# Turned probabilities through one PSUM bank, row sums by a column of ones, values in two banks

## The chip, the cores and the metric

The kernel runs on one core of one Trainium2 chip. The core has a matrix engine (PE, with its weight loads, PEld), a vector engine (DVE), a scalar engine (ACT), a general engine (Pool) and a DMA-issuing engine (SP); each takes its own instructions in order, and they wait for one another by semaphores. The metric is the time of one execution in microseconds; lower is better.

## The reference, cut to what matters

Two layers of gated cross attention, each with a mixture of experts behind it, on `x` (16 batches of 112 tokens, 256 wide) and a context of 375 keys per batch. The change lies in the first layer alone:

```
x = x + tanh(g_xattn[0]) * L0_xattn(layernorm(x), ctx, mask, ...)   # 16 heads of 16
    q = query @ Wq.T + bq ; k = key @ Wk.T + bk ; v = key @ Wv.T + bv
    scores = q * scale @ k.T + (1 - mask) * -10000
    probs  = softmax(scores)                 # over 375 keys
    ctx    = probs @ v                       # [112, 16] per head
x = x + tanh(g_ffn[0]) * L0_ffn(layernorm(x), ...)   # top 2 of 8 experts
```

The second layer (16 heads of 64 over 487 keys) and the last experts follow and are not touched.

## The kernel before, in words

The program has three stages, one after the other: small heads (with the first experts), large heads, and the experts of the second layer. The first, `phase_attention_small_heads`, runs over 16 batches, and each batch over 16 heads. One head is one slot `s` of the loop in `body`, which every engine has for itself. In slot `s` of batch `b`:

- PE: `scores(s)` into one of two banks `ps_s` (L593); `transposes(s-2)`, three fp32 transposes of 125 keys each of the probabilities into one of two banks `ps_t` (L602); `values(s-4)`, six products of turned probabilities and v, each split into a high and a low half in fp16, into the one bank `ps_o` (L616); then the slot's work items: projections of batch b+1 (`PSLOT`: keys in slots 0 and 1, turned tokens in 2, queries in 4, values in 5 to 7; L509, L531) and expert products of batch b-1 (`DSLOT`: slots 7 to 14, the four pairs of experts in 9, 10, 12 and 13; L509, L562, L569, L576).
- DVE: `maxima(s)` adds the mask, scales and takes the row maximum (L837); copies for the items; `plo(s-2)` writes the low half of the turned probabilities out of `ps_t` (L842).
- ACT: items; `exps(s-1)` (L701), with the row sum by the accumulator of the instruction; `phi(s-2)` writes the high half out of `ps_t` (L708).
- Pool: normalisation, splits of queries and context into halves, the residual, sums of experts, in one list per batch. SP: loads, the rearranging copies `stack_keys` and `mask_queries`, stores, in one list per batch.

Heads lag by slots, so in slot `s` a negative `s - lag` means a head of the batch before. `transposes(h)` wait for `exps(h)` and, for their bank, for `plo(h-2)`. `values(b, 0)` would fall in slot 4, but `ps_o` still holds batch b-1 until `read_out(b-1)` in slot 4; PE defers it to slot 5, which does two heads. `read_out` divides later by the sums that the accumulator gave. Batch 0 has no expert items; batches 14 and 15 have a copy of the next stage's weights (`next_high`) on ACT in half of their slots. After the last batch a short drain does the transposes and values that are left. The order of work is written out by hand.

Of the kernel before, what the change touches and what calls it, by code (L numbers as in the profile page):

```python
# [16 lines left out]
ALU = mybir.AluOpType  # L17
# [8 lines left out]
B = 16  # L26
T = 112
# [12 lines left out]
KB0, NB0 = 125, 3  # L40
SCALE0 = D0 ** -0.5
# [71 lines left out]
def phase_attention_small_heads(nc, x, ctxT, mask, g_xattn, g_ffn, wq, wk, wv, bq, bk, bv, wg, we, be, consts,  # L113
# [3 lines left out]
    with ExitStack() as ctx:  # L117
# [47 lines left out]
        v_s = [sb(f"v_s{i}", [128, NB0, H, 2, D0], F16) for i in range(2)]  # L165
# [3 lines left out]
        prob = sb("prob", [T, RING, C], F32)  # L169
        top = sb("top", [T, RING], F32)  # L170
        sums = [sb(f"sums{i}", [T, H], F32) for i in range(2)]
        pT = sb("pT", [128, RING, 2, NB0, 128], F16)
# [38 lines left out]
        s_blank = sem("blank")  # L211
# [80 lines left out]

        def heads(s, lag, b, par):

            h = s - lag
            return (b, par, h) if h >= 0 else (b - 1, 1 - par, h + H)


# [6 lines left out]
        def _(sp):  # L305
# [60 lines left out]
            def body(b, par):  # L366
                if ahead(b, 1):
                    load_mask(b + 1, 1 - par)
                if not first(b):
                    load_residual(b - 1)  # L370
                if ahead(b, 2):
                    load_tokens(b + 2)
                if ahead(b, 1):
                    stack_keys(b + 1, 1 - par)
                    mask_queries(b + 1, 1 - par)
                clear_rows(b)
                if not ahead(b, 1):
                    load_residual(b)
                if not first(b):
                    store(b - 1)  # L380
# [5 lines left out]
            sp.wait_ge(s_blank, 1)  # L386
            run_batches(sp, body)
            store(B - 1)
# [5 lines left out]
        def _(pool):  # L394
            pool.memset(be_f[:, :], 0.0).then_inc(s_zero, 1)
            pool.memset(blank[:, :], 0.0).then_inc(s_blank, 1)
# [4 lines left out]
            settled = (s_zero, 4)  # L401

            def split_context(c):

                need_all(pool, settled, (s_cload, 16, c, 16), (s_item, PI, c, 0))
                pool.tensor_copy(ctx_s[:, HI, :, :], ctx_f[:, :, :]).then_inc(s_csplit, 1)
                need(pool, s_csplit, 2, c, 1)
                pool.tensor_tensor(ctx_s[:, LO, :, :], ctx_f[:, :, :], ctx_s[:, HI, :, :], ALU.subtract).then_inc(s_csplit, 1)
# [26 lines left out]
            def residual(c):  # L435

                need(pool, s_rload, 16, c, 16)
                pool.tensor_tensor(x_b[:, :], x_res[:, :], bv_t[:, :], ALU.add).then_inc(s_xb, 1)
                need(pool, s_rsumt, 1, c, 1)
                need(pool, s_oread, 1, c, 1)  # L440
# [16 lines left out]
            def sum_experts(c, alone=True):  # L457

                for j in range(E // 2):
                    if not alone:  # L460
                        for n in range(2):
                            next_low((c - (B - 3)) * 8 + 2 * j + n)
                    need(pool, s_scaled, E // 2, c, j + 1)
                    need(pool, s_odd if j else s_x2, E // 2 if j else 1, c, j)
                    pool.tensor_tensor(acc_odd[:, :], scaled[j % 2][:, :], (acc_odd if j else x1)[:, :], ALU.add).then_inc(s_odd, 1)
# [5 lines left out]
            def body(b, par):  # L471
                if ahead(b, 1):
                    deviation_x(b + 1)
                if not first(b):
                    residual(b - 1)
                    deviation_x1(b - 1)
                if ahead(b, 1):
                    mask_bias(b + 1, 1 - par)
                    split_queries(b + 1)
                if ahead(b, 2):  # L480
                    split_context(b + 2)
                if not first(b):
                    sum_experts(b - 1, ahead(b, 2))
                if first(b):
                    for n in range(H // 2):
                        experts_low(n)

            split_context(0)
# [3 lines left out]
            split_context(1)  # L492
# [5 lines left out]
            run_batches(pool, body)  # L498
            residual(B - 1)
            deviation_x1(B - 1)  # L500
            sum_experts(B - 1)

        @block.tensor
        def _(pe):
# [14 lines left out]
            def item(c, par, k):  # L519
# [25 lines left out]
                else:  # L545
                    j = k - P_V
                    pe_wait_weights(c, 3)
                    last = product(ps[0:KB0, 0:D], lambda a, t: ctx_s[:, a, t, j * KB0:(j + 1) * KB0],
# [48 lines left out]
            def transposes(b, h):  # L597
                need(pe, s_exp, H, b, h + 1)

                need(pe, s_plo, H, b, h - 1)  # L600
                for j in range(NB0):
                    last = pe.transpose(ps_t[h % 2][0:KB0, j * T:(j + 1) * T],  # L602
                                        prob[:, h % RING, j * KB0:(j + 1) * KB0], ident[0:T, 0:T])
                last.then_inc(s_tr, 1)

            def values(b, par, h):
                need(pe, s_phi, H, b, h + 1)
                need(pe, s_plo, H, b, h + 1)
                if h == 0:
                    need(pe, s_oread, 1, b, 0)  # L610
                    need(pe, s_ihi, 6, b, 6)
                    need(pe, s_ifree, PI, b, PI)
                for j in range(NB0):
# [1720 lines left out]
```

## Time and profile before

| | us |
|---|---|
| median of 3 runs | 1444.75 |
| lowest, highest | 1437.92, 1447.92 |
| the profiled execution | 1443.42 |
| its span, first to last instruction | 1441.8 |
| PE busy | 1264.8 (88%) |
| DVE busy | 1092.9 (76%) |
| ACT busy | 1003.9 (70%) |
| Pool busy | 827.7 (57%) |
| granted PE clock, mean | 0.944 of full |

The time of an execution is a little more than the span of its instructions, and the profile is one execution; so a difference worked out from its rows is added to 1443.42, and the median of the runs lies 1.3 above that. The first stage takes the first 463 us or so of the span. Busy shares are means over stages with different limits.

### The profile page before, as it was taken

Reading aid. Unit: us, or ns where it says so; the run is one execution under the profiler, and the core shown is the slowest. Engines: PE = TensorE matmul, PEld = TensorE weight load, DVE = VectorE, ACT = ScalarE, POOL = GpSimd, SP = SyncE. Lnnn points to the kernel's source line nnn. Section 1 sums busy time; section 2 is a strip of 40 time slices with the busy share of each in tenths; the row PEclk is TensorE's granted clock in tenths of the full one; section 3 lists DMA queues with packets and bytes.
Section 4 is the critical chain, followed back from the end, with each engine's and each line's share of the span. In section 5 each row is a group of like instructions: output and inputs, shape, how many; then the busy total and the mean of one; then the engine's idle time right before and its main releaser. Section 6 shows DMA issues by size and latency. Waiting matters only on the chain. (4 is left out here: it accounts for less than half of the span.)

```text
span 1441.8 us, 44028 instructions
## 1 busy us (share of the span) xinstructions
PE 1264.8 (88%) x13508; PEld 916.7 (64%) x13508; DVE 1092.9 (76%) x3110; ACT 1003.9 (70%) x2584; POOL 827.7 (57%) x1204
## 2 busy tenths in 40 slices
PE   5999999999985599999998999999999985389994
PEld 3788888888864245656665556656566653278993
DVE  4899999999984268887887877878788873367772
ACT  3988788887883368787776777777787872155662
POOL 3645444454455445777676776777677675045663
PEclk9999999999997699999999999999999996599997
DMA  6233343333400148877666766767576784753323
GB/s 172 86 120 112 106 121 98 118 99 121 120 24 17 48 92 160 159 137 148 136 148 136 151 137 140 141 145 156 122 146 138 146 186 85 285 173 60 61 35 74
DMA packets 303968, 175.19 MB, mean 122 GB/s; under 512 B 250234, under 2 KB 291586, under 8 KB 300720
## 3 DMA queue, kind: packets, MB, share of 16 engines
q1 hardware_dynamic: 287632, 130.94, 40.8%
q0 software_dynamic: 13168, 35.80, 9.8%
q10 hardware_dynamic: 3024, 6.47, 1.6%
q8 instruction: 98, 1.61, 0.5%
q14 instruction: 46, 0.38, 0.1%
HBM read 64.48 MB, written 41.96 MB: 74 GB/s over the span
## 5 line engine op out<-in xcount | busy, mean ns | idle before, releaser
L1663 ACT ACTIVATE b_prob<-b_prob,b_top 112x487 f32<-112x487 f32 x256 | 178.9, 699 | 42.8 <-DVE b_top L1789 40.9
L1296 POOL TENSOR_TENSOR b_halves<-b_prob,b_halves 112x487 f16<-112x487 f32 x128 | 152.3, 1190 | 88.4 <-ACT b_halves L1688 86.6
L1474 PE MATMUL b_ps_p<-w_s,b_tok_s 128*128 128x512 f16 (+1 forms) x768 | 187.7, 381 | 5.6 <-DVE b_k_s L1776 5.3
L1474 PE MATMUL b_ps_p<-b_tok_s,w_s 128*128 128x487 f16 x768 | 188.0, 384 | 4.7 <-POOL b_tok_s L1290 3.7
L1789 DVE CUSTOM_DVE_ANT_0 b_prob<-b_ps_s,b_keep 112x487 f32<-112x487 f32 x256 | 167.7, 656 | 32.1 <-PE b_ps_s L1567 31.8
L701 ACT ACTIVATE a_prob<-a_prob,a_top 112x375 f32<-112x375 f32 x256 | 156.4, 611 | 4.5 <-DVE a_top L837 3.4
L1688 ACT ACTIVATE b_halves<-b_prob 112x487 f16<-112x487 f32 x256 | 156.0, 609 | 0.4
L837 DVE CUSTOM_DVE_ANT_0 a_prob<-a_ps_s,a_keep 112x375 f32<-112x375 f32 x256 | 138.6, 541 | 21.8 <-PE a_ps_s L593 19.2
L1582 PEld LDWEIGHTS b_ps_o<-b_v_s,b_pT 128*128 128x128 f16 (+1 forms) x3072 | 124.9, 100 | 32.7 <-DMA b_pT<-b_halves 11.0
L1582 PE MATMUL b_ps_o<-b_v_s,b_pT 128*128 128x64 f16 (+1 forms) x3072 | 136.1, 195 | 9.0 <-DMA b_pT<-b_halves 8.9
L842 DVE TENSOR_TENSOR a_pT<-a_ps_t,a_pT 125x336 f16<-125x336 f32 x256 | 128.6, 503 | 18.4 <-ACT a_pT L708 12.4
L602 PE MATMUL a_ps_t<-a_const,a_prob 112*125 112x112 f32 x768 | 127.8, 275 | 9.0 <-ACT a_prob L701 7.2
L602 PEld LDWEIGHTS a_ps_t<-a_const,a_prob 112*125 112x125 f32 x768 | 113.9, 189 | 31.3 <-ACT a_prob L701 22.5
L593 PE MATMUL a_ps_s<-a_k_stack,a_q_masked 128*112 128x375 f16 x512 | 126.5, 329 | 6.7 <-DMA a_q_masked<-a_q_s 6.1
L1474 PEld LDWEIGHTS b_ps_p<-b_tok_s,w_s 128*128 128x128 f16 x768 | 67.3, 100 | 96.4 <-issue 27.0
L1474 PEld LDWEIGHTS b_ps_p<-w_s,b_tok_s 128*128 128x128 f16 (+1 forms) x768 | 70.7, 105 | 85.1 <-DVE b_k_s L1776 14.1
L1776 DVE TENSOR_TENSOR b_k_s<-b_ps_p,b_k_s 128x487 f16<-128x487 f32 x128 | 84.5, 661 | 52.3 <-ACT b_k_s L1644 51.9
L1794 DVE TENSOR_TENSOR b_halves<-b_prob,b_halves 112x487 f16<-112x487 f32 x128 | 123.6, 965 | 0.0
L1567 PE MATMUL b_ps_s<-b_k_s,b_q_s 64*112 64x487 f16 x768 | 109.2, 391 | 14.8 <-issue 14.5
L708 ACT ACTIVATE a_pT<-a_ps_t 125x336 f16<-125x336 f32 x256 | 115.3, 450 | 9.8 <-PE a_ps_t L602 8.9
L1651 ACT ACTIVATE b_v_s<-b_ps_p 128x512 f16<-128x512 f32 (+1 forms) x128 | 76.2, 595 | 54.7 <-PE b_ps_p L1474 53.7
L1784 DVE TENSOR_TENSOR b_v_s<-b_ps_p,b_v_s 128x512 f16<-128x512 f32 (+1 forms) x128 | 87.9, 687 | 28.7 <-ACT b_v_s L1651 27.6
(262 smaller groups left out, 3063.0 us busy)
## 6 DMA issues: line engine op xcount, KB each, us to landing
xs<-a_blank SPq DMA_DIRECT2D x14, 1032.0 KB, 4.0
c_w_pool<-w_split SPq DMA_DIRECT2D x8, 1600.0 KB, 10.9
b_wch_f<-in_w_experts POOLq DMA_DIRECT2D x32, 384.0 KB, 4.9
w_split<-b_wch_s POOLq DMA_DIRECT2D x32, 384.0 KB, 4.0
a_ctx_f<-in_ctxT SPq DMA_DIRECT2D x16, 375.0 KB, 3.9
a_k_stack<-a_k_s SPq DMA_DIRECT2D x64, 93.8 KB, 2.8
b_ctx_t<-in_ctx SPq DMA_DIRECT2D x16, 375.0 KB
c_xt<-xs SPq DMA_DIRECT2D x35, 129.0 KB, 2.5
```

The source lines that it names most:

```text
L593: last = pe.matmul(ps_s[h % 2][0:T, 0:C], q_masked[par][:, part, m, g * T:(g + 1) * T], k_stack[par][:, g, :], start=(part == HI), stop=(p ...
L602: last = pe.transpose(ps_t[h % 2][0:KB0, j * T:(j + 1) * T], prob[:, h % RING, j * KB0:(j + 1) * KB0], ident[0:T, 0:T])
L701: act.activation(prob[:, h % RING, :], prob[:, h % RING, :], ACT.Exp, bias=top[:, h % RING:h % RING + 1], scale=-1.0, accum_out=sums[par][ ...
L837: dve.tensor_tensor_reduce(prob[:, h % RING, :], ps_s[h % 2][0:T, 0:C], keep[par][:, :], -SCALE0, 3e38, ALU.add, ALU.min, top[:, h % RING: ...
L842: dve.tensor_tensor(pT[0:KB0, h % RING, LO, :, 0:T], ps_t[h % 2][0:KB0, 0:NB0 * T].rearrange("p (j n) -> p j n", j=NB0), pT[0:KB0, h % RIN ...
L1296: pool.tensor_tensor(halves[:, h % TURN, LO, 0:NK], prob[:, h % RING, 0:NK], halves[:, h % TURN, HI, 0:NK], ALU.subtract).then_inc(s_lo[1], 1)
L1474: last = pe.matmul(out, sta(a, k), mov(m, k), start=(k == 0 and n == 0), stop=(k == tiles - 1 and n == 2))
L1582: last = pe.matmul(ps_o[h // 8][:, col:col + D1], pT[0:k, h % TURN, a, j, :], v_s[par][0:k, m, j, h * D1:(h + 1) * D1], start=(h % 8 == 0 ...
L1663: act.activation(prob[:, h % RING, 0:NK], prob[:, h % RING, 0:NK], ACT.Exp, bias=top[:, h % RING:h % RING + 1], scale=-1.0, accum_out=sums ...
L1688: act.activation(halves[:, h % TURN, HI, 0:NK], prob[:, h % RING, 0:NK], ACT.Copy).then_inc(s_hi, 1)
L1789: dve.tensor_tensor_reduce(prob[:, h % RING, 0:NK], ps_s[h % 3][0:T, 0:NK], keep[par][:, :], -SCALE1, 3e38, ALU.add, ALU.min, top[:, h % R ...
L1794: dve.tensor_tensor(halves[:, h % TURN, LO, 0:NK], prob[:, h % RING, 0:NK], halves[:, h % TURN, HI, 0:NK], ALU.subtract).then_inc(s_lo[0], 1)
```

## The change

- `ps_t` is one bank instead of two, and `transposes(h)` wait for `plo(h-1)`.
- `ps_o` is two banks of eight heads each. `values(h)` of all heads keep the lag of four slots; the first half of a batch is read in slot 15 (`out_lo(b, 0)` on ACT, `read_out(b, 0)` on DVE), the second in slot 4 of the next.
- `exps` write no row sum. `v_s` has a column of ones behind the low half of each head, and `values` move 33 columns instead of 32; the row sum is then column 32 of each head in `ps_o`, from which `read_out` takes the reciprocal.
- Keys are cut in blocks of 128, 128 and 119 instead of three of 125. The probabilities are padded with zeros to 384 and turned in three blocks of 128.
- `pT`, the turned probabilities, is a ring of eight heads instead of four.
- Pool's and SP's lists are put in slots. Pool: `residual_bias(b-1)` comes first, then `deviation_x`, `mask_bias`, the residual, `deviation_x1`, split queries, the two halves of the context split, the experts' sums. SP: mask, store of b-2, tokens of b+2, keys, masked queries, blank rows, residual of b.
- Four semaphores of the second stage (`turned`) are made outside it.

```diff
-        v_s = [sb(f"v_s{i}", [128, NB0, H, 2, D0], F16) for i in range(2)]
+        VW = 2 * D0 + 2
+        v_s = [sb(f"v_s{i}", [128, NA, H, VW], F16) for i in range(2)]
-        ps_t = [bank(f"ps_t{i}") for i in range(2)]
-        ps_o = bank("ps_o")
+        ps_t = bank("ps_t")
+        ps_o = [bank(f"ps_o{i}") for i in range(2)]
+        VSLOT = {s: [s - 4] for s in range(4, H + 4)}
...
@@ SP
-                if ahead(b, 1):
-                    load_mask(b + 1, 1 - par)
-                if not first(b):
-                    load_residual(b - 1)
-                if ahead(b, 2):
-                    load_tokens(b + 2)
...
+                for s in range(H):
+                    if s == 1 and ahead(b, 1):
+                        load_mask(b + 1, 1 - par)
+                    if s == 2 and not early(b, 2):
+                        store(b - 2)
+                    if s == 3 and ahead(b, 2):
+                        load_tokens(b + 2)
+                    if s == 5 and ahead(b, 1):
+                        stack_keys(b + 1, 1 - par)
+                    if s == 9 and ahead(b, 1):
+                        mask_queries(b + 1, 1 - par)
+                    if s == 11:
+                        clear_rows(b)
+                    if s == 13:
+                        load_residual(b)
@@ Pool
+                for s in range(H):
+                    if s == 0 and not first(b):
+                        residual_bias(b - 1)
+                    if s == 1 and ahead(b, 1):
+                        deviation_x(b + 1)
+                    if s == 2 and ahead(b, 1):
+                        mask_bias(b + 1, 1 - par)
+                    if s == 4 and not first(b):
+                        residual(b - 1)
...
@@ PE
             def transposes(b, h):
+                i = h
                 need(pe, s_exp, H, b, h + 1)
 
-                need(pe, s_plo, H, b, h - 1)
-                for j in range(NB0):
-                    last = pe.transpose(ps_t[h % 2][0:KB0, j * T:(j + 1) * T],
-                                        prob[:, h % RING, j * KB0:(j + 1) * KB0], ident[0:T, 0:T])
+                need(pe, s_plo, H, b, i)
+                for j in range(NA):
+                    last = pe.transpose(ps_t[:, j * T:(j + 1) * T],
+                                        prob[:, h % RING, j * KA:(j + 1) * KA], ident[0:T, 0:T])
                 last.then_inc(s_tr, 1)
...
+                if h % 8 == 0:
+                    need(pe, s_oread, 2, b - 1, h // 8 + 1)
-                        last = pe.matmul(ps_o[:, 32 * h:32 * h + 32], pT[0:KB0, h % RING, part, j, :],
-                                         v_s[par][0:KB0, j, h, :, :], start=(h == 0 and j == 0 and part == HI),
+                        last = pe.matmul(ps_o[h // 8][:, col:col + VW - 1], pT[0:r, h % TURN, part, j, :],
+                                         v_s[par][0:r, j, h, 0:VW - 1], start=(h % 8 == 0 and j == 0 and part == HI),
@@ ACT
-                               scale=-1.0, accum_out=sums[par][:, h:h + 1]).then_inc(s_exp, 1)
+                               scale=-1.0).then_inc(s_exp, 1)
...
+                    if s == H - 1:
+                        out_lo(b, 0)
@@ DVE
+                need(dve, s_olo, 2, c, i + 1)
+                dve.reciprocal(rsum[:, group], out[:, :, 2 * D0]).then_inc(s_rsum, 1)
...
+                    if s == H - 1:
+                        read_out(b, 0)
```

## Rows read from the trace of the kernel before

**Rows 1.** Busy us (and instructions) of each engine, granted clock; one batch.

```profile
core 0: us, PE busy (x) PEld busy (x) DVE busy (x) ACT busy (x) POOL busy (x), PEclk, DMA share, GB/s
232.24:257.83 25.59, 25.31 (x270) 21.07 (x269) 23.83 (x84) 21.08 (x67) 11.68 (x17) 1.00 0.40 121
```

**Rows 2.** Timeline of PE, the same batch: start, duration, line, operation, count, idle before.

```profile
232.24 0.48 PE L602 MATMUL a_ps_t<-a_const,a_prob 112*125 112x112 f32 x3
...
233.98 0.48 PE L602 MATMUL a_ps_t<-a_const,a_prob 112*125 112x112 f32 x3
...
237.41 0.51 PE L593 MATMUL a_ps_s<-a_k_stack,a_q_masked 128*112 128x375 f16 x2
238.00 0.58 PE L602 MATMUL a_ps_t<-a_const,a_prob 112*125 112x112 f32 x3
...
240.05 0.48 PE L602 MATMUL a_ps_t<-a_const,a_prob 112*125 112x112 f32 x3
...
248.41 0.48 PE L602 MATMUL a_ps_t<-a_const,a_prob 112*125 112x112 f32 x3
...
250.52 0.48 PE L602 MATMUL a_ps_t<-a_const,a_prob 112*125 112x112 f32 x3
...
251.45 0.48 PE L602 MATMUL a_ps_t<-a_const,a_prob 112*125 112x112 f32 x3
...
255.78 0.48 PE L602 MATMUL a_ps_t<-a_const,a_prob 112*125 112x112 f32 x3
...
257.83 0.55 PE L602 MATMUL a_ps_t<-a_const,a_prob 112*125 112x112 f32 x3
```

**Rows 3.** Timeline of all engines, the drain behind the last batch.

```profile
444.25 0.55 PE L602 MATMUL a_ps_t<-a_const,a_prob 112*125 112x112 f32 x3 [0.52 <-DVE a_pT L842]
...
444.84 0.45 ACT L708 ACTIVATE a_pT<-a_ps_t 125x336 f16<-125x336 f32 x1 [0.41 <-PE a_ps_t L602]
...
445.32 0.51 DVE L842 TENSOR_TENSOR a_pT<-a_ps_t,a_pT 125x336 f16<-125x336 f32 x1 [0.36 <-ACT a_pT L708]
...
445.97 0.30 PE L616 MATMUL a_ps_o<-a_v_s,a_pT 125*128 125x32 f16 x6 [0.56 <-DVE a_pT L842]
```

**Rows 4.** Timeline of DVE, slots 5 and 10 of the batch.

```profile
241.05 0.51 DVE L842 TENSOR_TENSOR a_pT<-a_ps_t,a_pT 125x336 f16<-125x336 f32 x1
...
248.71 0.55 DVE L837 CUSTOM_DVE_ANT_0 a_prob<-a_ps_s,a_keep 112x375 f32<-112x375 f32 x1 [0.21 <-PE a_ps_s L593]
...
250.60 0.50 DVE L842 TENSOR_TENSOR a_pT<-a_ps_t,a_pT 125x336 f16<-125x336 f32 x1
```

**Rows 5.** Timeline of ACT, slots 5 and 6 of the batch.

```profile
240.56 0.45 ACT L708 ACTIVATE a_pT<-a_ps_t 125x336 f16<-125x336 f32 x1 [0.48 <-PE a_ps_t L602]
240.91 1.08 ACT L665 ACTIVATE a_q_f<-a_ps_p,a_bq_c 128x112 f32<-128x112 f32 x4
...
242.71 0.48 ACT L708 ACTIVATE a_pT<-a_ps_t 125x336 f16<-125x336 f32 x1
```

**Rows 6.** Timeline of ACT, slot 1 and slot 14 of the batch.

```profile
235.01 0.44 ACT L708 ACTIVATE a_pT<-a_ps_t 125x336 f16<-125x336 f32 x1
...
256.61 0.19 ACT L701 ACTIVATION_READ_ACCUMULATOR a_prob<-a_prob,a_top 112x1 f32 x1
256.70 0.44 ACT L708 ACTIVATE a_pT<-a_ps_t 125x336 f16<-125x336 f32 x1
```

**Rows 7.** Timeline of PE, batch 15, slots with a weight copy on ACT.

```profile
415.58 0.58 PE L602 MATMUL a_ps_t<-a_const,a_prob 112*125 112x112 f32 x3 [0.37 <-ACT a_prob L701]
417.03 0.58 PE L602 MATMUL a_ps_t<-a_const,a_prob 112*125 112x112 f32 x3 [0.37 <-ACT a_prob L701]
```

**Rows 8.** Busy us by stretch, as in rows 1: batch 0, and batch 15.

```profile
40.00:52.00 12.00, 8.99 (x99) 6.19 (x97) 8.06 (x26) 12.00 (x34) 11.31 (x10) 1.00 0.31 110
...
427.80:433.00 5.20, 5.20 (x34) 4.38 (x35) 3.59 (x14) 2.43 (x7) 0.00 (x0) 0.53 0.00 0
```

**Rows 9.** Timeline of all engines, batch 15.

```profile
427.80 0.63 PE L562 MATMUL a_ps_p<-a_const,a_xn 112*128 112x112 f32 x2 [2.55 <-DVE a_xn L813]
...
428.22 0.83 PE L593 MATMUL a_ps_s<-a_k_stack,a_q_masked 128*112 128x375 f16 x2
```

More of the change, by code:

```diff
@@ L291, in phase_attention_small_heads @@
         WPARTS = ((512, 768), (0, 512), (768, 1024 + E))
+        VSLOT = {s: [s - 4] for s in range(4, H + 4)}
+        VALUES = tuple(range(H))
         def heads(s, lag, b, par):
@@ L385, in _ @@
             mask_queries(0, 0)
-            sp.wait_ge(s_blank, 1)
+            sp.wait_ge(s_zero, 2)
             run_batches(sp, body)
+            store(B - 2)
             store(B - 1)
@@ L455, in next_low, with add_expert, finish @@
                 pool.tensor_tensor(next_w[:, LO, cols], next_f[:, cols], next_w[:, HI, cols], ALU.subtract).then_inc(s_nlo, 1)
[L457 to L465, printed above, removed]
+            def add_expert(c, j, alone=True):
+                if not alone:
+                    for n in range(2):
+                        next_low((c - (B - 3)) * 8 + 2 * j + n)
+                need(pool, s_scaled, E // 2, c, j + 1)
+                need(pool, s_odd if j else s_x2, E // 2 if j else 1, c, j)
+                pool.tensor_tensor(acc_odd[:, :], scaled[j % 2][:, :], (acc_odd if j else x1)[:, :], ALU.add).then_inc(s_odd, 1)
+            def finish(c):
                 need(pool, s_odd, E // 2, c, E // 2)
@@ L471, in body @@
             def body(b, par):
-                if ahead(b, 1):
-                    deviation_x(b + 1)
-                if not first(b):
[L475 to L488, printed above, removed]
+                for s in range(H):
[7 more added lines that the diff above has]
+                        residual(b - 1)
+                    if s == 5 and not first(b):
+                        deviation_x1(b - 1)
+                    if s == 6 and ahead(b, 1):
+                        split_queries(b + 1)
+                    if s == 8 and ahead(b, 2):
+                        context_high(b + 2)
+                    if s == 10 and ahead(b, 2):
+                        context_low(b + 2)
+                    if s >= 12 and not first(b):
+                        add_expert(b - 1, s - 12, ahead(b, 2))
+                    if s >= 8 and first(b):
+                        experts_low(s - 8)
+                if not first(b):
+                    finish(b - 1)
+            context_high(0)
+            context_low(0)
             mask_bias(0, 0)
@@ L498, in _ @@
             run_batches(pool, body)
+            residual_bias(B - 1)
             residual(B - 1)
             deviation_x1(B - 1)
-            sum_experts(B - 1)
+            for j in range(E // 2):
+                add_expert(B - 1, j)
+            finish(B - 1)
         @block.tensor
@@ L630, in body @@
                     scores(b, par, s)
+                    c, _, h = heads(s, 2, b, par)
                     if not (first(b) and s < 2):
-                        c, _, h = heads(s, 2, b, par)
                         transposes(c, h)
-                    if s == 5:
-                        values(b, par, 0)
-                    if s != 4 and not (first(b) and s < 4):
-                        values(*heads(s, 4, b, par))
+                    for h in VSLOT.get(s + H, []):
+                        if not first(b):
+                            values(b - 1, 1 - par, h)
+                    for h in VSLOT.get(s, []):
+                        values(b, par, h)
                     if ahead(b, 1):
@@ L651, in _ @@
             run_batches(pe, body)
-            drain(B - 1, 1)
+            for s in range(H, H + 4):
+                if s - 2 < H:
+                    transposes(B - 1, s - 2)
+                for h in VSLOT[s]:
+                    values(B - 1, 1, h)
             for k in range(DI):
@@ L1114, in phase_attention_large_heads @@
         s_lo = [sem("lo_even"), sem("lo_odd")]
-        s_turned = [sem(f"turned{i}") for i in range(RING)]
         s_pv = sem("pv")
@@ L2273, in build_program @@
         s_rows = ctx.enter_context(nc.semaphore("rows"))
+        s_turned = [ctx.enter_context(nc.semaphore(f"turned{i}")) for i in range(4)]
         with nc.sbuf_tensor("w1_s", [128, 2, WKV + WQ + WOUT], F16) as w1_s:
```

136 lines of the change are left out of this document (72 added, 64 removed).

## The prediction

> **What bounds the kernel now.** I first looked in which stage the change lies: the small-head attention, whose loop over batches ends some 446 us into the span [rows 3]. The busy times of one batch in its middle [rows 1] say that of 25.59 us PE works 25.31, DVE 23.83, ACT 21.08, Pool 11.68, at full granted clock. So this stage is paced by PE, with DVE close behind, and the two later stages are unchanged. Then the timeline of PE through the same batch [rows 2]. One period is 257.83 - 232.24 = 25.59 us, the transposes of a batch standing there sixteen times. Take the time from the transposes of one slot to those of the next as the slot's length. It is 1.74 in slot 0 (slot 1 the same), 2.05 in slot 4, 2.11 in slot 10 (9 and 13 the same), but 0.93 in slot 11. All sixteen in order: 1.74, 1.75, 1.21, 1.06, 2.05, 1.63, 1.47, 1.67, 1.48, 2.11, 2.11, 0.93, 2.22, 2.11, 1.15, 0.90. What differs is the work item that PE does in the slot; without one, 0.8 to 1.0 is enough. PE can run that unevenly because `transposes(h)` needs only that `plo(h-2)` has read its bank: it is a whole slot ahead of the two copies that empty it.
>
> **The one bank for turned probabilities.** This is the term that decides. Now `transposes` of head h wait until `plo(h-1)` has ended, and that follows `phi(h-1)`, which follows the transposes of h-1. So transposes, copy on ACT, subtraction on DVE and again transposes form a closed ring, one head at a time. Its length can be read at the end of the stage, where nothing else is left to do [rows 3]: transposes start 444.25, `phi` 444.84 (0.59 later), `plo` 445.32 (0.48), the PE work that waits for it 445.97 (0.65). Sum 1.72 us. No slot can then be shorter than that; behind the transposes PE queues values, the work item and the next scores, and these are too little in nine of the sixteen slots (2, 3, 5 to 8, 11, 14, 15: together 11.50 us). 9 x 1.72 = 15.48, so 3.98 us more per batch.
>
> In five slots the ring holds other work of ACT or DVE too, since both are in order:
> - Slot 10: between the maxima and `plo` stand the small instructions that make the expert weights [rows 4]. Maxima start 0.30 after the transposes (they wait for scores there), `plo` 1.89 after that (250.60 - 248.71), next transposes 0.65 later: 2.84 instead of 2.11.
> - Slot 6: on ACT, `phi` of slot 5 to `phi` of slot 6 is 2.15 without a pause, for the four query copies and a value copy lie between [rows 5]. Less 0.09 (below), 2.06.
> - Slot 1: the key copy waits for PE's item of slot 0, and `phi` stands behind it, 1.03 after the transposes at 233.98 [rows 2, 6]: 1.03 - 0.09 + 0.48 + 0.65 = 2.07. In slot 2 the same copy is ready earlier, as slot 1 became longer.
> - Slot 14: `phi` behind an expert copy that waits for PE, 0.92 after the transposes at 255.78 [rows 2, 6]: 0.92 - 0.09 + 1.13 = 1.96.
> - Slot 5: the transposes come late, with their weights loaded; `plo` 1.00 later (241.05 - 240.05, [rows 2, 4]), + 0.65 = 1.65.
>
> The new batch: own length in slots 0, 4, 9, 12, 13: 1.74 + 2.21 + 3 x 2.11 = 10.28 (slot 4 takes over the values of head 0, which is 0.16; slot 12 loses a short wait). Ring alone in 2, 3, 7, 8, 11, 15: 6 x 1.72 = 10.32. With chains: 2.07 + 1.65 + 2.06 + 2.84 + 1.96 = 10.58. Sum 31.18, so **+5.6 us per batch**, and 13 batches give +72.7. Batch 0 has no expert items and batches 14 and 15 have a weight copy on ACT in half of their slots; there ACT already sets slots of 1.44 to 1.45 [rows 7], which the ring lengthens by 0.28. Batch 0: 8 x 0.28, and 2.0 for its slots 2 to 7, 4.2; batch 14: 2.0 for slots 0 to 7 and 2.2 for the rest, where ACT's copy is partly paid already; batch 15: 7 x 0.28, and 3 for slots 10, 11, 14 and 15 as in the middle; the drain 0.5. In all +87 us.
>
> **Row sums by a column of ones.** ACT no longer reads its accumulator after each exponential: 256 instructions of 0.19 us. They overlap their neighbours: in [rows 6] the read starts at 256.61 and `phi` at 256.70, so what the queue gets back is 0.09. Where ACT sets the pace (24 slots) it would be 2 us; behind the ring it is worth only the 0.09 used above. PE pays with 33 columns for 32, and the sums are read strided from PSUM: no row shows it; between 0 and, per batch, the 0.50 us that a whole `plo` takes from PSUM [rows 3], on DVE, in slots where DVE has room. I take 0.
>
> **Values in two banks.** PE need not defer head 0 from slot 4 to 5; work moves by 0.16 and none goes. The reading splits in two, and the first half comes in slot 15: a half copy on ACT, two more instructions on DVE, together below 0.5 us on DVE. It lies between the `plo` of slot 15 and of slot 0. There the ring leaves DVE 1.72 - 0.51 = 1.21 us, and maxima and the statistics take some 0.9. Just filled: 0 taken, up to 0.3 per batch kept for the range.
>
> **Blocks of 128.** Three transposes of 128 columns for 125, copies of as many elements per partition: 0. The memsets of the padding and the ones run on Pool before the first scores, while Pool waits for loads: 0, at most 1.
>
> **Pool and SP in slots.** Pool is 46% busy. Of what moves, only `residual_bias` goes ahead of `deviation_x`, 0.73 us before something that DVE wants a slot later. SP issues mask, tokens, keys and masked queries in the old order, the store ahead of the token loads, the residual at the end; each is due half a batch later. Behind the store, which waits for Pool's last sum, now stand the token loads; that sum is done by slot 0. 0, as slots grow longer; if something came late, PE might stand in each batch as it did once at 427.8, where a value of DVE came 2.55 us late [rows 9]: up to +40, for which nothing else in the trace speaks. The `turned` semaphores of the next stage are only declared elsewhere: 0.
>
> **Sum.** 1443.4 us (the profiled execution's own time, 1.6 above its span) + 87 = 1530. The median of the three runs is 1.3 above that execution: **1532 us**, 6% slower.
>
> A rule of the Trainium skill speaks against this edit: "Perfetto Trace Analysis", section Matmuls, wants independent matmul groups to rotate through PSUM banks, so that ACT and DVE empty one while the next is filled. The trace agrees as far as two banks go, by the waits for `plo`, nearly absent in the timeline; without that rotation the sum above is what results, with it about nothing. Against that, the Trainium skill reports in "TensorE: Matmul & The Clock Gate", section "HAM oscillation", that double buffering PSUM gave one kernel no further gain; by that the loss would be about zero, the rival "no slower" below. That kernel waited for something else; here the ring is longer than PE's work in nine slots.
>
> **Rivals.**
> - *Only the bare ring counts.* If the chains of slots 1, 6, 10 and 14 are absorbed (items can slip ahead when PE waits), each batch gets 4.1: +61 to 66, 1506. For it: queues do drain in longer slots. Against: slot 10's chain starts with scores that PE delivers late.
> - *The ring is longer.* Handovers of 0.1 more, the half reading in slot 15, a copy in the way in more slots: +0.15 per slot over 1.72 in ten slots and 0.3 once is +1.8 per batch, 1560. For: DVE has 23.8 us of work in a 25.6 us batch [rows 1] and meets the ring in any order. Against: 31 us give it slack.
> - *No slower.* The wait for the bank is hidden, because PE's queued work lasts as long as the two copies. The place is `transposes` in the light slots; it decides from a ring below 0.9 us. Then what is left are gains: the wait of slot 4 for exponentials, between 0 and the 0.59 from its scores (237.41) to its transposes [rows 2], times 16, and 0.09 in 24 slots. That is 0 to -11.6; half of it gives 1439, within 1%. Against it stands 1.72 by [rows 3]; it holds only if `plo` and the transposes are not tied as the diff says.
> - *The clock falls.* More pauses of PE might lower its granted clock from 2.4 to 1.2 GHz. After a pause of 2.55 us it was 0.53 for 5 us, and a pair of score products took 0.83 for 0.48 [rows 8, 9]. In slots of 1.45, with PE idle a quarter of the time, it stayed 1.00 [rows 8], and the ring leaves no pause above 1 us. If it fell, most of 25 us of PE work per batch would double: over +250, some 1700. The Trainium skill, "TensorE: Matmul & The Clock Gate", section "A second HAM failure mode: psum-queue depth-cycling", describes short pauses between groups that make the clock swing; by that rule it would be this rival. The trace does not bear it out.
>
> **How the numbers follow.** Ring with chains (1512 to 1552) 0.60; bare ring (1500 to 1512) 0.15; longer ring (above 1552) 0.12, half of it below 1560; part of the waiting hidden (1460 to 1500) 0.05; no slower 0.05; clock falls 0.03. From 1500 to 1560 lie 0.81. About 1% is what a measurement here can tell from no change. Slower by over 1%: 0.94; within 1%: 0.04; faster: 0.02.
>
> **What would show it.** After: PE's idle before the transposes, released by DVE `plo`, some 60 to 90 us in all where [rows 3] show a wait of 0.52; a period near 31 us; light slots at 1.7 between transposes; PE busy share about 82%, clock still 1.00; no accumulator reads. A period under 29 would refute the chains, one under 27 the ring. Another releaser ahead of the transposes or the scores (a load, Pool) would mean that the reordering costs.

## The result and the profile after

| us | before | after |
|---|---|---|
| median | 1446.34 (4 runs, 1437.92 to 1453.01) | 1530.40 (4 runs, 1526.70 to 1535.59) |
| profiled execution | 1443.42 | 1526.70 |
| its span | 1441.8 | 1525.1 |
| PE busy | 1264.8 (88%) | 1279.9 (84%) |
| DVE busy | 1092.9 (76%) | 1107.9 (73%) |
| ACT busy | 1003.9 (70%) | 993.9 (65%) |
| granted PE clock, mean | 0.944 | 0.943 |

After over before is 1.0587, 95% interval [1.0521, 1.0652]: 5.9% slower. All engines do nearly as much work as they did; the time is waiting. (The traced execution is the shortest of the four.) Three groups of the page say where it went (line, engine, operation, tiles, count | busy us, mean ns | idle us just before them, and what ended most of it):

```profile
L649 PE MATMUL a_ps_t<-a_const,a_prob 112*128 112x112 f32 x768 | 124.1, 271 | 82.8 <-DVE a_pT L894 66.0
...
L756 ACT ACTIVATE a_pT<-a_ps_t 128x336 f16<-128x336 f32 x256 | 114.8, 449 | 88.6 <-PE a_ps_t L649 88.4
...
L894 DVE TENSOR_TENSOR a_pT<-a_ps_t,a_pT 128x336 f16<-128x336 f32 x256 | 129.4, 505 | 52.7 <-ACT a_pT L756 47.1
```

The same group of the page of before:

```profile
L602 PE MATMUL a_ps_t<-a_const,a_prob 112*125 112x112 f32 x768 | 127.8, 275 | 9.0 <-ACT a_prob L701 7.2
```

Read the releasers: PE's transposes wait for DVE's `plo` (L894), `plo` for ACT's `phi` (L756), `phi` for the transposes (L649). Three engines wait for one another in turn, which is a closed ring, and PE's wait before the transposes went from 9.0 to 82.8 us. The busy times of one batch, to hold against [rows 1]:

```profile
311.05:342.28 31.23, 26.42 (x268) 19.47 (x268) 24.75 (x86) 20.10 (x51) 11.64 (x18) 1.00 0.27 82
```

The period is 31.23 us for 25.59, PE's work 26.42 for 25.31: PE stands for 4.8 us of this batch, and no other engine is busier than PE. The bare ring is purest at the start of the last batch, in this timeline of PE:

```profile
502.56 0.48 PE L649 MATMUL a_ps_t<-a_const,a_prob 112*128 112x112 f32 x3 [0.68 <-DVE a_pT L894]
...
504.21 0.48 PE L649 MATMUL a_ps_t<-a_const,a_prob 112*128 112x112 f32 x3 [0.68 <-DVE a_pT L894]
...
505.86 0.48 PE L649 MATMUL a_ps_t<-a_const,a_prob 112*128 112x112 f32 x3 [0.68 <-DVE a_pT L894]
...
507.52 0.48 PE L649 MATMUL a_ps_t<-a_const,a_prob 112*128 112x112 f32 x3 [0.68 <-DVE a_pT L894]
```

Transposes start every 1.65 us, each time released by `plo`. The turn of the ring in slot 11 of the batch above, over all engines (selected lines):

```profile
332.92 0.48 PE L649 MATMUL a_ps_t<-a_const,a_prob 112*128 112x112 f32 x3 [0.59 <-DVE a_pT L894]
...
333.43 0.45 ACT L756 ACTIVATE a_pT<-a_ps_t 128x336 f16<-128x336 f32 x1 [0.49 <-PE a_ps_t L649]
...
333.92 0.51 DVE L894 TENSOR_TENSOR a_pT<-a_ps_t,a_pT 128x336 f16<-128x336 f32 x1 [0.29 <-ACT a_pT L756]
...
334.57 0.48 PE L649 MATMUL a_ps_t<-a_const,a_prob 112*128 112x112 f32 x3 [0.56 <-DVE a_pT L894]
```

0.51 to `phi`, 0.49 to `plo`, 0.65 to the transposes: 1.65. In the drain of the kernel before the three were 0.59, 0.48 and 0.65 [rows 3]; the first is the shorter one. Slot 10 has its chain: behind the maxima stand the expert weights, ahead of `plo`.

```profile
330.08 0.45 PE L649 MATMUL a_ps_t<-a_const,a_prob 112*128 112x112 f32 x3
...
330.38 0.55 DVE L889 CUSTOM_DVE_ANT_0 a_prob<-a_ps_s,a_keep 112x375 f32<-112x375 f32 x1 [0.22 <-PE a_ps_s L639]
...
332.18 0.17 DVE L968 TENSOR_TENSOR a_cw<-a_picked 112x8 f32<-112x8 f32 x1
332.27 0.50 DVE L894 TENSOR_TENSOR a_pT<-a_ps_t,a_pT 128x336 f16<-128x336 f32 x1
```

The next transposes start at 332.92, so the slot lasted 2.84, the predicted number. `plo` started 1.89 after the maxima, as in [rows 4]; what is new is that PE must wait for it.

Where the 83 us lie: the second stage's first instruction starts at 556.60 for 465.11, which is 91.5 us later; what follows it took 968.5 us for 976.7, 8.2 less, though its code is the same. The later stages of the kernels below took 971 to 979 us, so this execution was short there. Of the 8.2, 6.8 lie in the second stage (757.9 us for 764.7), and there the granted clock stood at the lower of its two levels for 78.7 us instead of 88.9. Over the ten traces the stage tends to be longer where that time is longer (84.7 us low, 760.5 long; 88.6 and 764.5; 92.4 and 768.3; but also 92.6 and 765.0), so part of it is probably the clock; how much is not shown.

### The profile page after: what moved, and what is told of

Same layout as the page of the kernel before. It is cut to its first block and busy times, and to the rows that moved or that the text cites. A ratio compares the mean times of both kernels' runs of the same rounds, so it can differ in the third digit from the quotient of the medians.

```text
span 1525.1 us, 43858 instructions
## 1 busy us (share of the span) xinstructions
PE 1279.9 (84%) x13508; PEld 892.4 (59%) x13508; DVE 1107.9 (73%) x3142; ACT 993.9 (65%) x2344; POOL 829.9 (54%) x1207
## 5 line engine op out<-in xcount | busy, mean ns | idle before, releaser
L649 PE MATMUL a_ps_t<-a_const,a_prob 112*128 112x112 f32 x768 | 124.1, 271 | 82.8 <-DVE a_pT L894 66.0
L756 ACT ACTIVATE a_pT<-a_ps_t 128x336 f16<-128x336 f32 x256 | 114.8, 449 | 88.6 <-PE a_ps_t L649 88.4
L649 PEld LDWEIGHTS a_ps_t<-a_const,a_prob 112*128 112x128 f32 x768 | 83.7, 144 | 145.5 <-issue 78.4
L894 DVE TENSOR_TENSOR a_pT<-a_ps_t,a_pT 128x336 f16<-128x336 f32 x256 | 129.4, 505 | 52.7 <-ACT a_pT L756 47.1
L1530 PEld LDWEIGHTS b_ps_p<-b_tok_s,w_s 128*128 128x128 f16 x768 | 67.0, 99 | 94.9 <-issue 25.8
```

Source lines behind the costliest of these rows:

```text
L649: last = pe.transpose(ps_t[:, j * T:(j + 1) * T], prob[:, h % RING, j * KA:(j + 1) * KA], ident[0:T, 0:T])
L894: dve.tensor_tensor(pT[:, h % TURN, LO, :, 0:T], ps_t[:, 0:NA * T].rearrange("p (j n) -> p j n", j=NA), pT[:, h % TURN, HI, :, 0:T], ALU.s ...
L1530: last = pe.matmul(out, sta(a, k), mov(m, k), start=(k == 0 and n == 0), stop=(k == tiles - 1 and n == 2))
```

## The experiments

The medians of before in the runs that these kernels were set beside lie between 1439.8 and 1446.3; so the ratios are what is to be compared. "Period" is the time from the transposes of a slot to those of the same slot a batch later.

### One bank alone

```diff
-        ps_t = [bank(f"ps_t{i}") for i in range(2)]
+        ps_t = bank("ps_t")
-                need(pe, s_plo, H, b, h - 1)
+                need(pe, s_plo, H, b, h)
-                    last = pe.transpose(ps_t[h % 2][0:KB0, j * T:(j + 1) * T],
+                    last = pe.transpose(ps_t[0:KB0, j * T:(j + 1) * T],
```

made in the kernel before, and the same in the two copies that read the bank.

> The kernel before with one edit: the turned probabilities have one bank, and transposes wait for the low-half copy of the head before. Ring theory (the one bank carries the loss, all other parts of the change are near zero): the same light slots of 1.65 to 1.72 us and the chain in slot 10 of 2.84, and 0.09 more in the chains that run through ACT, since the accumulator is still read; a batch of 31 to 32 us, 1525 to 1545 us, ratio 1.055 to 1.07. Rival, the loss is shared (the ones column and the strided reads, the two reads of values, the order on Pool and SP cost a good part): 1480 to 1505 us.

Measured: 1547.67 us (1546.06 to 1548.80), ratio 1.0713 [1.0674, 1.0753]; the second stage starts at 566.57. The one edit does all of the loss, and 10 us more than the whole change, a little above the range expected. Its ring in slot 11, in the timeline of PE:

```profile
305.43 0.55 PE L602 MATMUL a_ps_t<-a_const,a_prob 112*125 112x112 f32 x3 [0.56 <-DVE a_pT L842]
...
307.16 0.55 PE L602 MATMUL a_ps_t<-a_const,a_prob 112*125 112x112 f32 x3 [0.57 <-DVE a_pT L842]
```

1.73, where the changed kernel has 1.65. So the rest of the change gives something back; the last two experiments look for it.

### Everything but the bank

Two banks of turned probabilities need the eighth bank back. Sixteen heads of 33 columns are 528, more than the 512 fp32 columns that the kernel gives a bank, so here the ones column and the second value bank are out as well; the sums come from the accumulator, and `values(b, 0)` is deferred to slot 5 again. Blocks of 128, the longer ring `pT` and the lists of Pool and SP in slots stay.

```diff
-        ps_t = bank("ps_t")
-        ps_o = [bank(f"ps_o{i}") for i in range(2)]
+        ps_t = [bank(f"ps_t{i}") for i in range(2)]
+        ps_o = bank("ps_o")
-        VSLOT = {s: [s - 4] for s in range(4, H + 4)}
+        VSLOT = {s: [s - 4] for s in range(5, H + 4)}
+        VSLOT[5] = [0, 1]
-                need(pe, s_plo, H, b, i)
+                need(pe, s_plo, H, b, i - 1)
-                               scale=-1.0).then_inc(s_exp, 1)
+                               scale=-1.0, accum_out=sums[par][:, h:h + 1]).then_inc(s_exp, 1)
```

> The changed kernel with two banks for turned probabilities again. Eight banks don't hold that and two banks of values, so the values are back in one bank and the row sums in ACT's accumulator; the blocks of 128, the ring of eight turned heads and the slots of Pool and SP stay. Ring theory: a batch of 25.6 us as before, 1438 to 1452 us. Rival, Pool's and SP's new order costs something: 1465 us or more, with a wait for Pool or a load ahead of PE.

Measured: 1441.64 us (1436.61 to 1445.27, 10 runs), ratio 0.9976 [0.9950, 1.0002]. The periods are 25.6 and 25.8 in turn, those of before 25.6 and 25.9; the second stage starts at 465.38 for 465.11. Blocks, lists in slots and the longer ring together cost nothing when there are two banks, and give nothing that can be told: the interval runs from 0.5% faster to no change.

### The missing bank taken from the scores

All of the change, ones column and value banks too, but it is the scores that have one bank, and the turned probabilities two.

```diff
-        ps_s = [bank(f"ps_s{i}") for i in range(2)]
-        ps_t = bank("ps_t")
+        ps_s = bank("ps_s")
+        ps_t = [bank(f"ps_t{i}") for i in range(2)]
-                need(pe, s_max, H, b, h - 1)
+                need(pe, s_max, H, b, h)
-                need(pe, s_plo, H, b, i)
+                need(pe, s_plo, H, b, i - 1)
```

> The changed kernel whole, but the bank that is missing is taken from the scores: two banks for turned probabilities, one for scores (scores of a head wait for the maxima of the head before). That ring is scores to maxima 0.62 us and maxima to scores about 0.65, near 1.27, against 1.65 to 1.72, and it has DVE's other work in it. Ring theory: light slots go from 0.9 to about 1.3, and slots where DVE is behind wait some tenths more; +1 to +3 us per batch, 1460 to 1495, taken 1470. Rival, a bank costs the same wherever it is taken: 1520 to 1540.

Measured: 1459.80 us (1457.96 to 1462.56), ratio 1.0106 [1.0067, 1.0146], just below the 1460 to 1495 expected. The period is 27.2. The chain of the scores' bank has two members, not three; from slot 15 to the next slot 0, with other work of DVE ahead of the maxima (timeline, PE and DVE, selected):

```profile
294.34 0.53 PE L639 MATMUL a_ps_s<-a_k_stack,a_q_masked 128*112 128x375 f16 x2
...
295.15 0.54 DVE L889 CUSTOM_DVE_ANT_0 a_prob<-a_ps_s,a_keep 112x375 f32<-112x375 f32 x1
...
295.62 0.08 DVE L889 DVE_READ_ACCUMULATOR2_ANT a_top<- 112x1 f32 x1
...
295.76 0.53 PE L639 MATMUL a_ps_s<-a_k_stack,a_q_masked 128*112 128x375 f16 x2 [0.46 <-DVE a_top L889]
```

Its light slots, which had been 0.9 to 1.2, are now 1.27 to 1.49, and most of the others are hardly longer than before. So the same change with the other bank given up loses 1.1%, not 5.9%. The ones column and the two value banks are in that 1.1%: with two banks for the turned probabilities they cost no more, unless something else in the change gives time back.

### The ring without DVE

In the changed kernel `plo` no longer reads the bank: it writes zeros times the high half, from a tensor of zeros in SBUF, so that DVE works as before and the transposes wait for `phi` alone. The low half of the probabilities is left out.

```diff
-                need(pe, s_plo, H, b, i)
+                need(pe, s_phi, H, b, i)
-                                  ps_t[:, 0:NA * T].rearrange("p (j n) -> p j n", j=NA),
-                                  pT[:, h % TURN, HI, :, 0:T], ALU.subtract).then_inc(s_plo, 1)
+                                  zeros[:, :].rearrange("p (j n) -> p j n", j=NA),
+                                  pT[:, h % TURN, HI, :, 0:T], ALU.mult).then_inc(s_plo, 1)
```

> The changed kernel, but DVE's copy no longer reads the bank: it writes zeros from a buffer of its own as the low half (so the low half of the turned probabilities is left out), as many elements per partition as before, and the transposes wait only for ACT's copy. The bank is still one. Ring theory: the ring is 0.52 (transposes to copy) + 0.45 (copy) + 0.15 (handover) = 1.12, and no chain of DVE is in it, so slot 10 falls to 2.1: a batch of 26 to 27.5 us, 1448 to 1475. Rival, it isn't the length of the ring but the work on DVE and ACT and their reads of PSUM that set the new batch: above 1500.

Measured: 1481.26 us (1480.15 to 1484.84), ratio 1.0258 [1.0217, 1.0298], 6 us above the range expected. The shortest slots are 1.11 to 1.19, slot 10 is 2.08 for 2.84, the period 27.9. The member taken out gave the most part of the loss back, as the ring says.

Part of what is left comes from the substitute. It has both sources in SBUF, and beside Pool it is no longer as fast as the copy that it stands for: of the copies between 100 and 400 us, the 81 that ran with Pool idle took at most 0.51 us, while 27 of the 91 that ran beside it took 0.6 to 0.93. In the changed kernel none of the 256 took more than 0.51. In slot 7 (timeline, selected):

```profile
314.68 0.56 POOL L460 CAST a_q_s<-a_q_f 128x448 f16<-128x448 f32 x1
314.70 0.90 DVE L896 TENSOR_TENSOR a_pT<-a_zeros,a_pT 128x336 f16<-128x336 f32 x1
...
315.32 1.18 POOL L462 TENSOR_TENSOR a_q_s<-a_q_f,a_q_s 128x448 f16<-128x448 f32 x1
...
315.53 1.12 DVE L866 TENSOR_SCALAR a_xn<-a_x,a_mv,a_rstd 112x256 f32<-112x256 f32 x1
...
316.79 0.38 PE L610 MATMUL a_ps_p<-a_const,a_xn 112*128 112x112 f32 x2 [0.67 <-DVE a_xn L866]
```

Behind the late copy the normalisation of the tokens (L866) falls beside Pool's next instruction; it takes 1.12 us for 0.40 in the changed kernel, and PE waits for it. In twelve of the batches slot 7 takes 2.52 to 2.56 for 1.67. In the last two batches, beside Pool's splitting of the next stage's weights, one copy took 4.76 us and one 7.45, and PE waited 2.30 and 5.19 for them:

```profile
468.60 7.45 DVE L896 TENSOR_TENSOR a_pT<-a_zeros,a_pT 128x336 f16<-128x336 f32 x1
```

An estimate from these numbers, 0.85 in each of twelve batches and 7.5 at the end, is some 18 us, and 1481 less 18 is within the 1448 to 1475 expected. So this run shows that DVE's part of the ring matters, and how much only by that estimate.

### Expert weights behind the copy

In slot 10 of the changed kernel the small instructions come after `plo`.

```diff
-                        if s == 10:
-                            combine_weights(b - 1)
...
                         plo(c, h)
+                    if not first(b) and s == 10:
+                        combine_weights(b - 1)
```

> The changed kernel; in slot 10 DVE makes the expert weights behind the low-half copy instead of ahead of it. Chain theory (in a slot, what DVE and ACT have in their queues ahead of their copy adds to the ring, whoever put it there): slot 10 falls from 2.84 to 2.1 or 2.2, but the weights are then ready later, ACT's first expert copy of slot 11 stands ahead of its copy of turned probabilities, and slot 11 grows from 1.65 to about 2.9: +0.5 us per batch, 1530 to 1545. Rival (slot 10's loss belongs to slot 10 and is gone when the work is moved): -0.7 us per batch, 1515 to 1521.

Measured: 1541.86 us (1537.28 to 1545.81), ratio 1.0702 [1.0667, 1.0737]. The chain is real, and it moved. Transposes of slots 10, 11 and 12, timeline of PE:

```profile
336.14 0.45 PE L649 MATMUL a_ps_t<-a_const,a_prob 112*128 112x112 f32 x3
...
338.23 0.45 PE L649 MATMUL a_ps_t<-a_const,a_prob 112*128 112x112 f32 x3
...
341.07 0.58 PE L649 MATMUL a_ps_t<-a_const,a_prob 112*128 112x112 f32 x3 [1.14 <-DVE a_pT L894]
```

Slot 10 fell from 2.84 to 2.09, slot 11 rose from 1.65 to 2.84: +0.44 in the two, 7 us in 15 batches. A slot without work of its own now waits for the chain, where PE's pair of experts had covered 2.11 of it. In front of slot 12 PE stands for 1.14, and there the clock fell (busy us of PE, PEld, DVE, ACT, Pool; granted clock; DMA):

```profile
340.00:345.00 5.00, 3.93 (x20) 2.55 (x20) 2.45 (x7) 2.07 (x7) 1.37 (x2) 0.66 0.13 49
```

The slot behind it took 3.73 us for 2.11. The clock fell eight times in the batches of this kernel between 60 and 500 us, and three times in those of the changed one, where a fall cost 1.1 to 1.5 us; periods vary between 31.2 and 33.8 us, and the second stage starts 12.0 us later, not 7.

### Two of three blocks copied

`phi` and `plo` of the changed kernel copy 224 elements per partition for 336; PE's work stays. The last 119 keys are left out of the values.

```diff
-                act.activation(pT[:, h % TURN, HI, :, 0:T],
-                               ps_t[:, 0:NA * T].rearrange("p (j n) -> p j n", j=NA), ACT.Copy)
+                act.activation(pT[:, h % TURN, HI, 0:2, 0:T],
+                               ps_t[:, 0:2 * T].rearrange("p (j n) -> p j n", j=2), ACT.Copy)
```

and the same for `plo`.

> The changed kernel, but ACT's and DVE's copies take only two of the three turned blocks (the probabilities of the last 119 keys are left out; they stay zero), the PE work is whole. It shortens the ring by about 0.12 on either engine, 1.65 to 1.40, and nothing else. Ring theory: 0.25 less in each of the slots that the ring or a chain through both copies sets (some 10 of 16): -2.5 us per batch, slots of 1.40 in the timeline, 1485 to 1500. Rival (the loss comes with the wait itself, whatever the length of the copies): above 1520.

Measured: 1497.19 us (1496.11 to 1498.75), ratio 1.0390 [1.0367, 1.0413]. One turn of its ring:

```profile
312.02 0.48 PE L650 MATMUL a_ps_t<-a_const,a_prob 112*128 112x112 f32 x3 [0.47 <-DVE a_pT L895]
...
312.53 0.36 ACT L757 ACTIVATE a_pT<-a_ps_t 128x224 f16<-128x224 f32 x1 [0.37 <-PE a_ps_t L650]
...
312.92 0.39 DVE L895 TENSOR_TENSOR a_pT<-a_ps_t,a_pT 128x224 f16<-128x224 f32 x1
...
313.46 0.48 PE L650 MATMUL a_ps_t<-a_const,a_prob 112*128 112x112 f32 x3 [0.36 <-DVE a_pT L895]
```

1.44 for 1.65: `phi` is 0.09 shorter and `plo` 0.12, 0.21 in all, and slots 3, 5, 11 and 15 of the batch fell by just that, as did those of the chains through both copies, 1 and 14. Slots 6, 8 and 10 fell by half of it, 0.10 to 0.12. The rest stayed, slot 7 (1.67) too: that one is PE's own length, not the ring's. The period is 29.6 and 30.1 in turn, for 31.2 and 31.6, so 1.5 to 1.6 less and not the 2.5 expected: it is 0.21 in some seven and a half slots, not 0.25 in ten. The median is in the range also because the clock did not fall in the batches before the last, as it did four times in the changed kernel. What the two copies lose in length, the ring loses one for one.

### One bank, no accumulator

The kernel of the first experiment without `accum_out`; the sums are a constant, so the normalisation by row sums is left out.

```diff
-                               scale=-1.0, accum_out=sums[par][:, h:h + 1]).then_inc(s_exp, 1)
+                               scale=-1.0).then_inc(s_exp, 1)
```

> The kernel before with one bank for turned probabilities, as in e1, and without the row sums (the accumulator isn't read, the division is by a constant). It separates the 17 us between e1 and the changed kernel. If they are the accumulator's read (0.09 of ACT's queue in each chain, so 0.5 to 0.6 us per batch) and what it does to PE's pauses: 1530 to 1540, near the changed kernel. If they are the values in two banks or the new order on Pool and SP: 1543 to 1550, as e1.

Measured: 1538.85 us (1537.70 to 1542.70), ratio 1.0691 [1.0663, 1.0718] beside 1.0713 [1.0674, 1.0753] with the accumulator. The intervals overlap; the periods don't: 31.6 and 31.7 for 31.9 and 32.0, so 0.28 us per batch: 0.09 in each of slots 1, 6 and 14, whose chains run through ACT. The second stage starts at 561.17 for 566.57. The median lies within the range expected for "it is the accumulator", but by the rows it is not: the gain per batch is half of what was expected there, the ratio is still 1% above the whole change's, and the slots of the bare ring stay at 1.72. The accumulator is not what made them 1.65.

### Blocks of 125

All of the changed kernel, with three blocks of 125 keys.

```diff
-KA, NA = 128, 3
+KA, NA = 125, 3
-                    last = pe.transpose(ps_t[:, j * T:(j + 1) * T],
+                    last = pe.transpose(ps_t[0:KA, j * T:(j + 1) * T],
```

> The changed kernel, whole, but with its keys cut in three blocks of 125 again instead of 128, 128 and 119; nothing is left out. The question is where 0.07 us of each ring went: 1.65 between transposes in the changed kernel where the drain of the kernel before showed 1.72, while the kernel before with one bank alone still shows 1.72 (305.43 to 307.16). There each of the three weight loads of a turned head takes 188 ns on the mean, in the changed kernel 142 ns, and the three transposes together 0.55 and 0.48 us. Theory A, the width of the block: loads of 125 columns are slower than loads of 128, and the three stand in the ring. Then the slots set by the bare ring are 1.72 again, the chains 0.03 to 0.07 longer, the period 31.23 + 0.4 to 0.7, thirteen to sixteen times, so a profiled span of 1531 to 1537, and a median of 1534 to 1542 (0.3 to 0.7 per cent over the changed kernel). Theory B, something else of the change (the accumulator's absence, the order in which values are done): slots stay at 1.65, the median within 1528 to 1533.

Measured: 1542.28 us (1538.53 to 1546.98), ratio 1.0680 [1.0640, 1.0720] for 1.0587 [1.0521, 1.0652] of the whole change. The median is at the upper end of theory A's range, the profiled span, 1542.5, above it. The intervals overlap at their ends; the periods don't: 31.8 and 32.2 in most batches for 31.2 and 31.6. The slots of the bare ring are 1.72 and 1.73 again, and the second stage starts at 564.91 for 556.60. The cause is one row in each kernel, the weight loads of the transposes, grouped from 100 to 490 us. The changed kernel, then this one:

```profile
L649 PEld LDWEIGHTS a_ps_t<-a_const,a_prob 112*128 112x128 f32 x593 | 64.1, 142 | 105.3 <-issue 53.3 <-ACT a_prob L749 44.9 <-DVE a_pT L894 2.9
```

```profile
L649 PEld LDWEIGHTS a_ps_t<-a_const,a_prob 112*125 112x125 f32 x578 | 81.5, 189 | 98.1 <-issue 47.8 <-ACT a_prob L749 44.2 <-DVE a_pT L894 3.2
```

A load of 125 columns takes 189 ns, one of 128 only 142. Two banks hide that, as "everything but the bank" showed (141 ns there for 188 before, and no gain); in the ring it is 0.07 per turn.

## Why the prediction was right, and where it was not

The forecast was 1532 us, the median is 1530.4. The mechanism was right: one bank closes a ring of three engines, and with the chains in it that is the loss. The nearness of the number is in part luck, so each term by itself:

- **The ring**, 1.72 by the drain: it is 1.65, because blocks of 128, put at nothing, load faster. With blocks of 125 it is 1.72 to 1.73, as read. The term "blocks of 128: 0" was the one mis-sized: it gives back about 0.56 us per batch under one bank (31.4 against 32.0, means of the two periods that alternate), while with two banks it is indeed 0.
- **The slots** of the batch above, in us:

  | slot | 0 | 1 | 2 | 3 | 4 | 5 | 6 | 7 | 8 | 9 | 10 | 11 | 12 | 13 | 14 | 15 | sum |
  |---|---|---|---|---|---|---|---|---|---|---|---|---|---|---|---|---|---|
  | predicted | 1.74 | 2.07 | 1.72 | 1.72 | 2.21 | 1.65 | 2.06 | 1.72 | 1.72 | 2.11 | 2.84 | 1.72 | 2.11 | 2.11 | 1.96 | 1.72 | 31.18 |
  | measured | 1.75 | 2.06 | 1.72 | 1.65 | 2.26 | 1.63 | 2.08 | 1.67 | 2.10 | 2.11 | 2.84 | 1.65 | 2.11 | 2.08 | 1.96 | 1.56 | 31.23 |

  The chains of slots 1, 6, 10 and 14 came as read. Slot 15 came out shorter than the ring, since the transposes behind it started 0.56 after `plo` and not 0.65; why is open.
- **The chain of slot 8 was missed.** PE's item of slot 7 stands behind transposes that now wait, so ACT's value copy comes late, and `exps` and `phi` queue behind it:

```profile
325.56 0.38 ACT L727 ACTIVATE a_v_s<-a_ps_p 119x256 f16<-119x256 f32 x1 [0.39 <-PE a_ps_p L554]
...
325.84 0.35 ACT L733 ACTIVATE a_x1T<-a_ps_p 128x224 f16<-128x224 f32 x1
...
326.07 0.61 ACT L749 ACTIVATE a_prob<-a_prob,a_top 112x375 f32<-112x375 f32 x1
...
326.57 0.45 ACT L756 ACTIVATE a_pT<-a_ps_t 128x336 f16<-128x336 f32 x1
...
327.33 0.50 DVE L894 TENSOR_TENSOR a_pT<-a_ps_t,a_pT 128x336 f16<-128x336 f32 x1
```

  The transposes stood at 325.87, `phi` came 0.70 after them for 0.51, and between it and `plo` DVE had its maxima and a value copy: 2.10. A slot's chain was looked for in the order of before, where that item came early. It cost +0.38, and slots 3, 7, 11 and 15, shorter than predicted (-0.35 together), hid it in the sum.
- **The stage.** From slot 0 to slot 0: batches 1 to 13 grew by 78.9 (predicted 72.7), batch 0 by 5.7 (4.2), batch 14 by 3.9 (4.2), batch 15 by 2.6 (5), the drain by 0.4 (0.5). Predicted +87 up to the second stage, measured +91.5. Of the 6.2 too little in the middle, the clock is some 5: batches 1, 2, 10 and 12 are 1.1 to 1.5 us longer than others of their kind, and they are the four in which the granted clock was down (46.4 to 60.1, 97.6 to 101.0, 350.2 to 353.6 and 415.1 to 418.5 us). The first of these falls also lengthened the last slots of batch 0, to 1.97. Batch 15 lost less since its old self already had the pause of 2.55 and the low clock behind it [rows 8, 9]: that slot took 4.33 us and takes 3.07 now.
- **After the stage**, 0 predicted, -8.2 found, explained in part at best. So the traced execution, 1526.7 for the 1530 worked out, hides 4.5 us too little in the stage behind 8 us too much after it; by its own terms the prediction was 4 to 5 us low.
- **Accumulator, ones column, value banks.** The accumulator was put at 0.09 in the chains alone, and that is what it is: 0.28 per batch. The changed kernel with blocks of 125, which has neither, is no shorter than one bank alone (32.0 and 31.9), so ones column and value banks cost about as much again, within the range kept for them. It shows in slot 4, which does the values of head 0 now: 2.26, and 1.89 with one bank alone, where they stay in slot 5. Only the sum was tried, not each.
- **Pool and SP in slots**: 0 predicted, and "everything but the bank" shows 0 together with the blocks and the longer ring `pT`.
- **The rivals.** The bare ring alone is refuted by slots 1, 6, 10 and 14, and by the chain that moved with the expert weights. The longer ring is refuted by 1.65. "No slower" fell with the result. "The clock falls" is right in kind and small: some 5 us in the batches, not 250. The prediction said there that the ring leaves no pause above 1 us; it left one of 1.15 in batch 0, ahead of 43.97 in the timeline of PE, and the clock fell 2.4 us after that pause.

The Trainium skill, "Perfetto Trace Analysis", section Matmuls, asks for a rotation through banks; the runs agree, with 7.1% for that edit alone. The remark of the Trainium skill in "TensorE: Matmul & The Clock Gate", section "HAM oscillation", that a second buffer gave no further gain does not carry over to a kernel whose bank is held by a ring of three engines.

## What to carry to other kernels

A buffer that one engine fills and two others empty in turn is a closed ring when there is only one: its length can be read wherever the kernel drains, and every slot with less work than that pays the difference, plus whatever in-order work lies inside the ring. If a bank must be found, take it from the shortest ring: here the scores' bank cost 1.1% where the turned probabilities' cost 5.9%. And cost small terms again once a buffer is gone, because what two banks hide (the width of a weight load, an accumulator read) costs time inside the ring. And look at a substitute in an experiment as closely as at the original: the one here, with both operands in SBUF, stood beside Pool as the original never did.

## What was not expected of the hardware

- **A weight load of 128 fp32 columns is faster than one of 125**: 142 ns for 189 in the two rows above, and 188 in the kernel before. The Trainium skill, "TensorE: Matmul & The Clock Gate", section "Weight-path perf modes", has a fast load for 128 weights, but not for FP32 input; for these fp32 transposes a load of 128 is a quarter shorter all the same. Whether it is that fast load, no run here shows.
- **What makes the clock fall is not plain from PE's pauses.** Batch 0, then the start of batch 15 of the changed kernel:

```profile
42.00:46.00 4.00, 2.18 (x28) 1.54 (x28) 2.70 (x9) 3.76 (x8) 3.73 (x4) 1.00 0.21 46
46.00:50.00 4.00, 3.05 (x28) 2.04 (x27) 1.94 (x6) 2.93 (x6) 3.69 (x4) 0.55 0.82 301
50.00:54.00 4.00, 3.37 (x30) 2.13 (x28) 1.94 (x6) 2.93 (x6) 2.38 (x3) 0.50 0.02 4
502.00:506.00 4.00, 2.09 (x24) 1.48 (x25) 2.90 (x10) 3.79 (x9) 2.07 (x3) 1.00 0.20 57
```

  Before the fall PE was busy for 2.18 of 4 us, in the other stretch for 2.09. In the first stretch the clock went from 2.4 to 1.2 GHz and stayed there to 60.1 us, and slots of the ring took 1.97 for 1.65; in the second it stayed at 2.4. The first stretch has a pause of 1.15 us, the second none above 0.68:

```profile
43.97 0.48 PE L649 MATMUL a_ps_t<-a_const,a_prob 112*128 112x112 f32 x3 [1.15 <-DVE a_pT L894]
```

  That pause does not decide it alone. The kernel with two of three blocks copied has one of 1.15 us too, at 41.5, and its clock stayed at 2.4 GHz up to 483.8 us; and at 97.6, 350.2 and 415.1 us the changed kernel's clock fell with no pause above 0.8 in the 7 us before. Once the batches had begun, none of the kernels with two banks for the turned probabilities showed a fall before the last two batches, and neither did the two with the shortest rings (1.12 and 1.44). What decides is open.
- **DVE can stand for microseconds beside Pool when its operands lie in SBUF**: the multiplication by zeros, both sources in SBUF, took 0.50 us in the median, 0.90 in the fence above and 7.45 at most; the subtraction of the changed kernel, one source in PSUM, took at most 0.51 in 256 copies, 116 of them beside Pool.
